# Macaron block on one core: second FFN's routing one iteration sooner in the mixer, seven blocks in it, four blocks' shared expert behind the routed ones

## What is computed

```python
x = x + 0.5 * ffn(layernorm(x))        # first FFN
x = x + mixer(layernorm(x))            # state space mixer with its own gated MLP
x = x + 0.5 * ffn(layernorm(x))        # second FFN, the same weights

def ffn(x):                            # D=128, HIDDEN=256, 8 experts, top 2
    shared = (silu(x @ sw1) * (x @ sw2)) @ sw3
    w, idx = top_k(softmax(x @ rw + rb), 2);  w = w / sum(w)
    return shared + sum over the 2 experts e of a token:
                    w_e * ((silu(x @ ew1[e]) * (x @ ew2[e])) @ ew3[e])
```

## Time and profile before

| | us |
|---|---|
| median of 3 runs | 753.91 (753.42 to 755.28) |
| the profiled execution, its own time | 755.59 |
| its span, first to last instruction | 753.9 |
| TensorE busy | 627.0 (83%) |
| VectorE busy | 558.6 (74%) |
| GpSimd busy | 529.1 (70%) |
| ScalarE busy | 384.7 (51%) |
| mean granted clock of TensorE | 0.930 |

### The profile page before, as it was taken

How to read it: one execution, slowest core, us unless ns; L and a number is a source line. 1 busy time by engine, 2 the same in 40 slices (tenths; PEclk the granted TensorE clock), 3 DMA queues, 4 the chain that set the end, 5 groups by cost and what they waited for, 6 DMA issues and landing times.

```text
span 753.9 us, 13811 instructions
## 1 busy us (share of the span) xinstructions
PE 627.0 (83%) x4044; PEld 482.2 (64%) x4044; DVE 558.6 (74%) x1728; ACT 384.7 (51%) x731; POOL 529.1 (70%) x668
## 2 busy tenths in 40 slices
PE   3378859999942578999999999899988979999981
PEld 2245539999941245656666666576854659999960
DVE  4665745877738979896989898999874546777738
ACT  1122224555522889685868677564312225655535
POOL 3777766777764876895978778876685744777750
PEclk9998998999985779989999999998999999999996
DMA  9511223333316000000000000000001133333318
GB/s 262 180 44 54 89 63 89 96 96 105 88 30 219 1 0 1 1 2 0 1 2 1 2 8 9 15 15 22 20 27 34 49 119 84 105 98 99 91 46 296
DMA packets 40249, 48.29 MB, mean 64 GB/s; under 512 B 7750, under 2 KB 33716, under 8 KB 40176
## 3 DMA queue, kind: packets, MB, share of 16 engines
q1 hardware_dynamic: 31088, 30.47, 13.8%
q0 software_dynamic: 9088, 16.94, 7.0%
HBM read 26.10 MB, written 23.10 MB: 65 GB/s over the span
## 4 chain that ended last, share of the span: by engine, by line
PE 39%; POOL 26%; issue 16%; DVE 11%; ACT 5%; DMA 3%; POOLq 0%; DVEq 0%; SPq 0%; ACTq 0%
POOL xs L728 13%; POOL ys L744 6%; PE ps_tr L1740 5%; PE ps_go L2130 5%; PE ps_go L1740 3%; PE ps_go L1911 2%; PE ps_go L1915 2%; PE ps_a L2116 2%; PE ps_tr L1928 1%; PE ps_a L2118 1%; PE ps_a L2117 1%; PE ps_b L2116 1%; PE ps_b L2118 1%; PE ps_b L2117 1%; PE ps_tr L2101 1%
## 5 line engine op out<-in xcount | busy, mean ns | idle before, releaser
L744 POOL DMA_INDIRECT ys<-arena,dest x156 | 153.0, 981 | 64.7 <-issue 44.6
L728 POOL DMA_INDIRECT xs<-rows,pos x128 | 127.4, 996 | 58.7 <-issue 42.4
L2130 PE MATMUL ps_go<-w_down_e,hid 128*128 x624 | 82.7, 275 | 1.2 <-DVE hid L1581 1.2
L2130 PEld LDWEIGHTS ps_go<-w_down_e,hid 128*128 128x128 f32 x624 | 76.5, 192 | 1.6 <-issue 1.6
L1054 ACT ACTIVATE xt_hi<-ps_tr 128x256 fp32r<-128x256 f32 x78 | 29.9, 384 | 55.7 <-PE ps_tr L2101 55.7
L1061 ACT ACTIVATE up_now<-up_hi 128x512 fp32r x78 | 48.6, 625 | 4.4 <-issue 3.4
L2116 PE MATMUL ps_a<-xt_hi,up_now 128*128 128x256 f32 x160 | 49.6, 310 | 0.8 <-DVE xt_lo L1561 0.7
L1581 DVE TENSOR_TENSOR hid<-silu_a,ps_a 128x512 f32<-128x512 f32 x40 | 27.5, 688 | 30.6 <-ACT silu_a L1070 30.6
L1042 ACT ACTIVATE silu_a<-ps_a 128x512 f32<-128x512 f32 x32 | 19.1, 597 | 55.8 <-PE ps_a L2080 54.7
L2116 PE MATMUL ps_b<-xt_hi,up_now 128*128 128x256 f32 x152 | 46.4, 306 | 0.0
L2117 PE MATMUL ps_a<-xt_lo,up_now 128*128 128x256 f32 x160 | 46.1, 288 | 0.0
(11 more groups left out here) (353 smaller groups left out, 1938.4 us busy)
## 6 DMA issues: line engine op xcount, KB each, us to landing
arena<-xs SPq DMA_DIRECT2D x78, 130.0 KB
rows<-ys SPq DMA_DIRECT2D x8, 512.0 KB, 3.7
arena<-ys SPq DMA_DIRECT2D x8, 512.0 KB, 7.4
ys<-arena,dest POOLq DMA_INDIRECT x156
xs<-fill SPq DMA_DIRECT2D x17, 130.0 KB, 2.9
x<-in_L_attn_x SPq DMA_DIRECT2D x8, 256.0 KB, 4.5
arena<-in_L_ffn_ew SPq DMA_DIRECT2D x4, 512.0 KB, 7.0
xs<-rows,pos POOLq DMA_INDIRECT x128, 2.4
```

Source lines behind the costliest of these rows:

```text
L728: pool.indirect_dma_start(xs, bass.IndirectOffsetOnAxis(pos[:, n, i:i + 1], 0), rows[:, n * TT + i % TT, :], None).then_inc(scattered, 16)
L744: pool.indirect_dma_start(ys, bass.IndirectOffsetOnAxis(dest[:, i:i + 1], 0), y_out[:, p % YRING, j, :], None, bounds_check=2 * TOK - 1, o ...
L2130: r = pe.matmul(ps_answers(p)[:, j * P:(j + 1) * P], hid_e(p)[:, at:at + P], w_down_e[:, bass.ds(which[p], 1), k, :].rearrange("p a d -> p ...
```

## The change

- `EARLY` 5 to 7: blocks 0 to 6 are routed inside the mixer's pipeline, and block 7 behind it.
- Logits, choice, rank, places and scatters of a block stand one iteration sooner in the lists: TensorE's `route_logits` goes from the start of the body at(−9) to behind `outputs(0)` at(−8), after the block's transposes in the same iteration; `route_rank` at(−8); VectorE's `route_choice` and `route_places` at(−7), in the iteration of `route_rows`; GpSimd's `route_scatter` at(−8). Their places within the list stay otherwise. The guards of reused PSUM banks are shifted to match.
- `LATE` 2 to 4, so `AHEAD` 6 to 4: blocks 0 to 3 have their shared expert ahead of the routed ones, 4 to 7 behind.
- `dve_ffn_again` writes block 7's normed rows first, before the first product of the shared expert.
- VectorE does all late blocks before the first finish, and ScalarE all late blocks before it scales any answer.

```diff
-EARLY = 5
+EARLY = 7
-LATE = 2
+LATE = 4
...
     # GpSimd, body
-                do(route_scatter, early(at(-9)), 0)
+                do(route_scatter, early(at(-8)), 0)
                 do(route_rstd, at(-7))
-                do(route_scatter, early(at(-9)), 1)
+                do(route_scatter, early(at(-8)), 1)
...
@@ act_late
-                if n > AHEAD:
-                    act_finish(act, n - AHEAD - 1)
-            for n in range(LATE - 1, NB):
+            for n in range(NB):
                 act_finish(act, n)
...
     # VectorE, body
-                do(route_choice, early(at(-8)))
+                do(route_choice, early(at(-7)))
...
-                do(route_places, early(at(-8)))
+                do(route_places, early(at(-7)))
...
@@ dve_ffn_again
             dve.wait_ge(mixer_done, NB)
+            dve_norm(dve, NB + NB - 1)
             for n in range(AHEAD + 1):
...
-                if n == 0:
-                    dve_norm(dve, NB + NB - 1)
...
             dve_ffn_again(dve, own)
-            dve_late(dve, AHEAD)
+            for n in range(AHEAD, NB + 1):
+                dve_late(dve, n)
             for n in range(NB):
-
-                if AHEAD + n < NB:
-                    dve_late(dve, AHEAD + n + 1)
                 dve_finish(dve, own, n)
...
@@ TensorE: guards, one block later each, as in
-                after(pe, rank_read, NB + min(n - 3, EARLY))
+                after(pe, rank_read, NB + min(n - 2, EARLY))
...
     # TensorE, body
-                do(route_logits, early(at(-9)))
...
                 do(outputs, at(-5), 0)
+                do(route_logits, early(at(-8)))
...
-                do(route_rank, early(at(-9)))
+                do(route_rank, early(at(-8)))
```

More of the change, by code:

```diff
@@ L679, in body @@
                 do(h_add, at(-5))
-                do(route_scatter, early(at(-9)), 2)
+                do(route_scatter, early(at(-8)), 2)
                 do(dt_sum, at(-2))
                 do(bc_spread, at(-3))
-                do(route_scatter, early(at(-9)), 3)
+                do(route_scatter, early(at(-8)), 3)
                 do(gated_output, at(-4), 0)
@@ L1833, in token_major @@
                     after(pe, silu_z_done[0], min(n + 2, NB))
-                    after(pe, logits_read, NB + min(n - 3, EARLY))
+                    after(pe, logits_read, NB + min(n - 2, EARLY))
                 if k == 0:
@@ L1953, in gate_up @@
                     after(pe, silu_g_done, FC * (n - 1) + 3)
-                    after(pe, logits_read, NB + min(n - 2, EARLY))
+                    after(pe, logits_read, NB + min(n - 1, EARLY))
                 if c == 2:
@@ L1986, in route_logits @@
                 n = SQ * b + q
-                after(pe, silu_z_done[0], min(n + 6, NB))
-                after(pe, hf_ready, min(FC * (n + 2) + 2, FC * NB))
+                after(pe, silu_z_done[0], min(n + 5, NB))
+                after(pe, hf_ready, min(FC * (n + 1) + 2, FC * NB))
                 pe_route_logits(pe, n, pb["rl"])
@@ L1993, in route_rank @@
                 n = SQ * b + q
-                after(pe, tm_ready, min(TT * (n + 4) + 3, TT * NB))
-                after(pe, mix_read, min(n + 4, NB))
+                after(pe, tm_ready, min(TT * (n + 3) + 3, TT * NB))
+                after(pe, mix_read, min(n + 3, NB))
                 pe_rank(pe, NB + n, pb["rk"])
```

## The result

| | before | after |
|---|---|---|
| median of the runs, us | 754.38 in this comparison (753.91 above) | 770.0 (768.1 to 774.0, 4 runs) |
| ratio | | 1.022, 95% interval 1.018 to 1.026 |
| span of the profiled execution | 753.9 | 768.8 |
| granted clock of TensorE | 0.930 | 0.920 |

The change makes the kernel 2.2% slower. Slower was forecast, but 757.4 was 12.6 us too low, and 770.0 lies outside the range.

The account below looks back on a forecast made before the run. Before the first tile GpSimd's scatters were last, TensorE's shared expert 3.3 us behind; in the mixer, waits over several engines. Terms 3.4 + 0.2 + 6.7 − 20.0 + 13.2 = +3.5 gave 757.4 us, range 753.3 to 761.5.

Parts of the forecast that it names:

- M: End of the mixer's last addition, 571.8 us before; forecast to come 6.7 later from blocks 5 and 6.
- steps 3 and 4: Mixer's end to first tile: shared expert becomes last, −20.0; four late blocks behind the expert tiles: +13.2.
- Step 1: Full mixer iterations: choice and scatter one iteration sooner cost +3.4, with later full iterations unchanged.
- A: Mixer iteration of 36.21 us without routing choice or scatter; gets one choice, forecast +1.10.
- B: Next mixer iteration, 37.31 us with one choice; gets one block's scatters too, forecast +2.34.
- C: Mixer iteration after B, 39.65 us with one choice and one block's scatters; forecast unchanged.
- a5: Start of the mixer's addition of block 4; from last u projection 30.7 us before, 30.9 forecast.
- Step 2: Mixer's drain: down projections wait behind the routing of blocks 5 and 6, +6.7, bounds 3 to 10.
- a7: Start of the mixer's addition of block 6; stretch from the previous addition 16.6 us before, 19.6 forecast.
- a8: Start of the mixer's last addition, block 7; stretch from the previous addition 9.6 us before, 13.3 forecast.
- Rival C: TensorE at half clock after the mixer-end holes: two stretches lose 3.4 us, 760.8 in all; chance 0.18.
- the sum's own case: Whole kernel: the steps' sum holds, 757.4 us, by itself 755.5 to 759.5; chance 0.50.

Follow-up runs that it names:

- no_collide_after: Changed kernel with `pos` written directly by the reduction, without the cast, and the small `bc_n` operation moved to GpSimd: 768.1 us, ratio 1.017.
- shift_only: Changed kernel with EARLY = 5, LATE = 2 and the old order of finishes, leaving only routing one iteration sooner: 760.6 us, ratio 1.007.
- adds_first_3: Changed kernel with blocks 5 and 6's transposes and logits behind the down projection, VectorE's last two additions ahead of the choice: 768.8 us, ratio 1.019.
- no_collide_before: Kernel before with `pos` written directly by the reduction, without the cast, and the small `bc_n` operation moved to GpSimd: 753.6 us, ratio 0.997.

## Why the prediction was wrong, by its own steps

- *What bounds the kernel, steps 3 and 4, and the direction* were right. M to the first tile: 29.1 against 29.4, a change of −20.3 against −20.0, released by the shared addition. The late part: +13.1 in the profile, from its first up projection to the last finish, against +13.2, and 768.3 in a run of its own.
- *Step 1* failed in size: it put +3.4 where the mixer lost 8.9. A was right (+1.2 for 1.10). B was taken as what C had been (+2.34) and cost +5.0; about 2.6 of that is the hole from one collision and the half clock behind it, shown by no_collide_after. That B without it is 39.7, the forecast figure, is partly luck: the 2.34 was put down mostly to two held-up instructions, and when both were taken away C fell by 0.65 only. The cast's 2.53 us is also longer than the 1.28 of the multiply beside it, so a hold-up is not bounded by that one GpSimd instruction, as the prediction had it. "Later full iterations keep one choice and one scatter each" was the sentence that failed: the last u projection to a5 cost +2.7, with the down projection at 4.65 us, and shift_only has the same. In adds_first_3 this stretch took 30.7, as before, with its down projection at 2.95; its C was 1.4 longer instead. So the clock is the likely cause of these 2.7, and no run took it away there alone. The wait that comes before it, 0.84 us for the logits' copy, is one that the change itself puts ahead of the down projection.
- *Step 2* is the step that failed most. It was right in its mechanism and its order, and about right in size for the clock it assumed: 6.7 forecast, 6.1 measured when fillers kept TensorE's clock up. What failed is its price for TensorE's work behind the new holes, 0.95 us for logits and 2.94 for a down projection, taken from rows at full clock. In after they took 1.85 and 4.87 to 5.09, the same step cost 11.8, and the half clock behind the holes of blocks 5 and 6 is 5.7 us of it. By the place of the excess: 5.0 instead of 3.1 at a7, 6.8 instead of 3.7 at a8.
- *Rival C* was this cause, priced at 3.4 us and given 0.18. It said that new holes bring 0.50 and counted two stretches of 1.7. The holes brought 5.7 in the drain. In the iterations ahead one brought 2.6 together with its collision, and the 2.7 ahead of a5 are likely the clock's too. The row at 0.50 in 574 to 576 stood behind two waits of TensorE of 1.39 and 0.78 us, shorter than the waits that the change brings (3.12 and 1.89 in after's drain). Against it, the row at 556.79 stood behind a wait of 1.34 at full speed. So the trace before showed both outcomes, and the work behind the new holes should have been priced at both levels, with the half clock in the sum's own case and the range wide enough for either. The Trainium skill, TensorE: Matmul & The Clock Gate, Part 1, says that an array that sat idle is back at 1.2 GHz until it has been busy again: the trace agrees with the two levels, 1.85 us for logits that take 0.95.
- *Sum.* Span +14.9 against +3.5: B 2.7, the stretch to a5 2.5, blocks 5 and 6 5.1 too low, 0.8 ahead of A, and the rest within 0.5.

The Trainium skill, SBUF — State Buffer, section Who interferes with whom, counts `tensor_scalar` among the operations that can enter a two-port mode, in which it and a GpSimd instruction block each other. The 1.77 us of a 128x8 `tensor_scalar` in B agree: it ended at 442.34, as the GpSimd multiply beside it did (442.29). The same instruction took 0.16 to 0.40 us in some iterations and 1.23 to 1.78 in the others. Removing it removed the hole in B.

## What to carry to other kernels

When work is moved into a stretch bound by a chain over four engines, price the work behind each new TensorE hole at the 1.2 GHz rows of the trace too, in the forecast itself and not in a rival; with the three prices that the runs gave afterwards (2.6, 2.6 and 5.7) the forecast of 757.4 would have been 768.3. It is a price to expect, not a certain one: the same hole left the clock full in other executions and kernels. If such a hole can't be avoided, idle matmuls in it are worth a try: here they gave back 7 of the 16 us at the usual level, and nothing where the kernel before took 845. Taking away one hold-up on VectorE did little for the whole: it came back at another instruction or in another iteration. An item moved in one engine's list does nothing while another engine's list keeps the old order, and moving it in both may only carry the hole past the mark one is looking at. A load shifted between two places that are rivals for one stretch (scatters, shared expert) has to be counted with the other one fixed and moved.

## What the runs showed of the hardware

- In after, holes of 1.77 to 3.12 us on TensorE were followed by 0.50 to 0.58 granted clock over 6 to 7 us; a 24-matmul down projection then took 4.87 to 5.09 us instead of 2.94. One of 0.84 us was too (4.65), and a hole of 2.16 in adds_first_3 was not (2.92).
- Where in the pipeline the clock falls is sensitive to shifts of a microsecond or two: the 2.6 us taken out of B came back in A and ahead of a5. In two executions of one kernel the same wait of 1.9 us left the clock at half (down projection 5.09) and at full (2.92).
- VectorE instructions of 0.16 to 0.31 us took 1.2 to 2.5 beside GpSimd's work, and with it taken away another one did (0.29 to 1.67, 0.31 to 2.06 in no_collide_before).
- The same chip ran the kernel before at 845 us once and at 755 another time. The kernel of adds_first took 857.1 and 768.8 there, with equal iterations in the mixer (B 42.8 and 42.4, C 41.0 and 41.1) and equal full-clock instructions (the down projection 2.94 in both).
- The best versions, no_collide_before and the one with block 5 in the mixer, are 0.3% faster than the kernel before, at the edge of what can be measured.
